# Rearranging all engines' work in the attention periods, the router stage and the first expert tile of a fused attention and mixture-of-experts kernel

## The chip, the cores and the metric

One core of a Trainium2 chip runs the whole kernel in one launch. The metric is the device time of that launch in microseconds. The kernel before takes 535.85 us, the median of three runs (535.5 to 536.07).

The core has engines that run side by side and meet only at semaphores: TensorE (PE; matrix products, transposes; writes only to PSUM banks), VectorE (DVE), ScalarE (ACT), GpSimd (POOL) and SyncE (SP), which here issues most of the transfers. Each engine works through its own list in order. A wait in such a list holds up everything behind it.

## The reference

Two steps are added to a residual stream `x` of 4 batches x 512 tokens x 512 channels. `ctx` holds 128 features for each token, `topk` keeps 153 of 512 values in a row.

```
sim  = (ctx @ Wq.T) (ctx @ Wk.T).T / scale            # per batch, 512 x 512
A    = sigmoid(sim) * (sim >= 153rd largest of its row)
x    = x + tanh(g1) * ((1-gamma) * layernorm(x) + gamma * (A + A.T) / 2)
xf   = layernorm(x)
shared = (silu(xf @ Gs.T) * (xf @ Ys.T)) @ Ds.T       # 704 hidden
s    = sigmoid(xf @ gate.T); two experts of 8 by s + bias, weights s/sum
out  = sum over the two: w_e * (silu(xf @ Ge.T) * (xf @ Ue.T)) @ De.T   # 352 hidden
x    = x + tanh(g2) * (shared + out)
```

`topk` must be exact, and the products are made to about float32's accuracy from pairs of float16 values, a high and a low half: high x high, high x low, low x high.

## The kernel before

The 2048 tokens are cut into 4 batches of 4 row tiles of 128. There is a prologue (attention of batch 0), then three calls of `together(b, more)`, one in each engine's list, then a last period with the router, then 39 expert tiles of 128 gathered token slots. In period `b` TensorE computes batch b's router logits (`logits`), its shared hidden blocks u = 0 to 5 (`shared_up`, 24 products of 512 columns each, 12 in block 5), and its shared down products (`shared_down`, one row tile at a time). Among these are the matrix turns for batch b + 1: `turn_attention` (the masked scores, which waits for `a_made`), `turn_batch` (a normalised row tile with its high and low half, into one of two banks, so tile 2 needs the bank of tile 0), and for batch b + 2 `project` and `scores`.

VectorE's list in period b: four rounds of a search for each row's threshold (`search`; ScalarE's `count` does half of the rows), exact thresholds by one more count and the eight largest below it (`last_counts`, `thresholds`), `count_missed`, `masks` (four `keep` instructions), `check`, which reads how many rows the search missed, branches to an exact fallback if there are any, and releases `a_made`; in between it multiplies the hidden blocks (`shared_hidden`, which frees TensorE's banks: block u + 2 waits for hidden block u). The first two base sums (`add_base`: gain x row + masked scores) stand inside `check` ahead of the branch. Then `attended` adds the turned scores, takes statistics, and makes the low half of each normalised row.

Weights arrive as 80 pieces of 128 x 544 float32 in a ring of four stage buffers (SP's `load_piece`, which waits until the low half of the piece four before is done). ScalarE makes the high half and scales the stage in place (`high_piece`), GpSimd or, for the last four experts, VectorE makes the low half (`low_piece`). `SLOT_PIECES` says how many pieces are handled at each hidden block u of periods 0 to 2. `high_piece` for slot u stands between the silu and the high half of block u or behind them, so a missing load holds ScalarE up with all its other work. GpSimd also makes the low half of each hidden block (`shared_low`) and the few scalars of a batch (`base_scalars`, `row_scalars`, `guess`).

In the last period VectorE chooses the experts (`choose`), counts (`count_tokens`), places the slots (`place`), builds one-hot matrices in eight steps (`hot_slots`), whose products with TensorE (`slots`) give the index table (`table`); `tile_experts` computes which expert each tile belongs to, and by how much the waits of the adding transfers count. GpSimd gathers four tiles' rows when `table` has released them. In an expert tile t ScalarE and VectorE alternate (silu, product, high half, low half), and in tiles 0 to 6 each converts four more weight pieces, two ahead of the high half and two at the end (`late_pieces`). TensorE's `turn_and_up` turns tile t - 1's hidden halves in the middle of tile t's products. The order of everything is written out by hand.

## Time and profile before

| | |
|---|---|
| median of three runs | 535.85 us |
| the profiled execution | 535.06 us, span 533.3 us |
| TensorE busy | 486.4 us, 91% of the span |
| VectorE, ScalarE, GpSimd busy | 327.7 us (61%), 254.3 us (48%), 220.4 us (41%) |
| transfers | 61.58 MB, mean 115 GB/s |
| share of the chain that ended last | TensorE 49%, VectorE 33%, ScalarE 5% |

TensorE's share is a mean over the whole span. The question in each stage is which wait ends last there. An order-of-time row has the start, the duration, the engine, the line of the kernel, the operation, what it writes and reads, and how many instructions it joins; square brackets hold the idle time of the engine ahead of it and who ended it. Rows of the same engine may overlap a little, since instructions are pipelined.

### The profile page before, as it was taken

How to read it: one execution, taken by the hardware profiler on the slowest of the kernel's cores; microseconds unless marked ns; L12 is line 12 of the kernel's file. 1: busy time of each engine (PE TensorE's matmuls, PEld its weight loads, DVE VectorE, ACT ScalarE, POOL GpSimd, SP SyncE). 2: the span in 40 equal slices, each digit the busy share in tenths (PEclk: the TensorE clock that was granted, in tenths of full speed). 3: DMA queues.
4: the chain of work that ended last, by engine and by line, in shares of the span. 5: the costliest groups of instructions: out<-in, count | busy, mean ns of one | idle time of the engine just before them, and what ended most of it. 6: DMA issues, size and time to landing. Idle time of an engine off the chain costs nothing.

```text
span 533.3 us, 10457 instructions
## 1 busy us (share of the span) xinstructions
PE 486.4 (91%) x2992; PEld 267.0 (50%) x2993; DVE 327.7 (61%) x726; ACT 254.3 (48%) x465; POOL 220.4 (41%) x229
## 2 busy tenths in 40 slices
PE   7467998999898997899889999999999999999991
PEld 2234433544344443454445666666666666666650
DVE  2999897899958995779976773323323233333330
ACT  3874696789389856532313653222222222222230
POOL 2022467616863296402430434443344443344322
PEclk9758798999999998999999999999999999999997
DMA  6430333354434442240056896566655666655643
GB/s 203 150 104 2 121 99 89 85 181 142 125 84 136 161 115 59 108 136 2 0 191 226 220 258 130 101 107 118 114 103 98 111 102 115 114 101 107 104 56 39
DMA packets 45478, 61.58 MB, mean 115 GB/s; under 512 B 20544, under 2 KB 20800, under 8 KB 45440
## 3 DMA queue, kind: packets, MB, share of 16 engines
q1 hardware_dynamic: 36272, 40.53, 25.7%
q0 software_dynamic: 8736, 20.45, 22.0%
q8 instruction: 18, 0.29, 0.2%
q10 hardware_dynamic: 432, 0.13, 0.1%
q14 instruction: 20, 0.16, 0.1%
HBM read 37.90 MB, written 19.14 MB: 107 GB/s over the span
## 4 chain that ended last, share of the span: by engine, by line
PE 49%; DVE 33%; issue 7%; ACT 5%; POOL 2%; DMA 2%; DVEq 0%; POOLq 0%; ACTq 0%
PE py L1153 14%; PE pg L1133 13%; PE pu L1134 13%; DVE w L1253 5%; PE pa L1143 2%; DVE work L1421 2%; DVE pa L1283 2%; DVE w L1310 2%; PE pt_bank L909 2%; DVE w L1300 2%; DVE w L1232 2%; DVE w L1287 1%; ACT w L688 1%; DVE w L1625 1%; DVE w L1359 1%
## 5 line engine op out<-in xcount | busy, mean ns | idle before, releaser
L1133 PE MATMUL pg<-w,x_t 128*128 x408 | 123.3, 313 | 0.0
L1134 PE MATMUL pu<-w,x_t 128*128 x408 | 123.2, 313 | 0.0
L580 POOL DMA_INDIRECT out<-rows,idx x39 | 61.8, 1586 | 134.3 <-issue 80.1
L975 PE MATMUL pg<-w 128*128 128x512 f16 x288 | 81.5, 402 | 6.0 <-DVE work L1421 6.0
L1153 PE MATMUL py<-w,work 128*128 x351 | 82.1, 379 | 0.8 <-DVE work L1688 0.8
L832 ACT ACTIVATE work<-pg 128x352 f32<-128x352 f32 x39 | 18.1, 463 | 120.0 <-PE pu L1134 120.0
L516 POOL TENSOR_TENSOR w<-stage,w 128x544 f16<-128x544 f32 x42 | 54.2, 1303 | 37.2 <-ACT stage L637 30.2
L975 PE MATMUL pu<-w 128*128 128x512 f16 x240 | 66.7, 388 | 0.0
L633 ACT ACTIVATE w<-stage 128x544 f16<-128x544 f32 x80 | 50.9, 648 | 28.3 <-DMA stage<-in_weights 28.0
L1677 DVE SCALAR_TENSOR_TENSOR work<-pu,work 128x352 f32<-128x352 f32 x39 | 20.4, 524 | 62.2 <-ACT work L832 56.8
L1688 DVE COPY work<-pa 128x768 f16<-128x768 f16 x39 | 21.8, 558 | 59.6 <-PE pa L1143 51.5
L1153 PEld LDWEIGHTS py<-w,work 128*128 128x128 f16 x351 | 34.3, 98 | 37.1 <-issue 1.2
L975 PEld LDWEIGHTS pg<-w 128*128 128x128 f16 x288 | 28.8, 102 | 42.2 <-issue 6.2
L1133 PEld LDWEIGHTS pg<-w,x_t 128*128 128x128 f16 x408 | 39.9, 98 | 17.5 <-issue 0.2
L530 POOL TENSOR_TENSOR work<-work 128x512 f16<-128x512 f32 x20 | 28.0, 1399 | 49.9 <-ACT work L714 49.9
L1134 PEld LDWEIGHTS pu<-w,x_t 128*128 128x128 f16 x408 | 39.9, 98 | 17.1
L975 PEld LDWEIGHTS pu<-w 128*128 128x128 f16 x240 | 23.9, 100 | 29.8 <-issue 2.7
L1253 DVE TENSOR_SCALAR_CACHE_REDUCE w<-w 128x512 f16<-128x512 f32 x48 | 33.9, 743 | 2.4 <-DVE w L1249 1.2
L1683 DVE TENSOR_TENSOR work<-work 128x352 f16<-128x352 f32 x39 | 20.4, 524 | 21.2 <-ACT work L837 21.2
L842 ACT ACTIVATE rows<-py,w_slot 128x512 f32<-128x512 f32 x39 | 26.8, 687 | 13.9 <-PE py L1153 13.9
L837 ACT ACTIVATE work<-work 128x352 f16<-128x352 f32 x39 | 19.3, 495 | 23.3 <-DVE work L1677 23.3
L1000 PE MATMUL pu<-w,work 128*128 128x512 f16 x120 | 27.8, 379 | 2.0 <-DVE w L1427 1.3
(250 smaller groups left out, 782.0 us busy)
## 6 DMA issues: line engine op xcount, KB each, us to landing
stage<-in_weights SPq DMA_DIRECT2D x80, 272.0 KB
xn_rows<-w SPq DMA_DIRECT2D x16, 256.0 KB, 2.8
out<-w SPq DMA_DIRECT2D x16, 256.0 KB, 2.5
w<-in_x SPq DMA_DIRECT2D x3, 1024.0 KB, 5.3
w<-in_ctx_t SPq DMA_DIRECT2D x4, 256.0 KB, 3.8
w<-in_x SPq DMA_DIRECT2D x2, 512.0 KB, 3.8
out<-rows,idx POOLq DMA_INDIRECT x39, 5.1
work<-xn_rows,idx POOLq DMA_INDIRECT x20
```

The source lines that it names most:

```text
L516: pool.tensor_tensor(w[:, ds(item, 1), 1, n * CHUNK_W:(n + 1) * CHUNK_W], stage[:, n % RING:n % RING + 1, :], w[:, ds(item, 1), 0, n * CHU ...
L530: pool.tensor_tensor(hid_tb[:, u, 1, :], hb[:, u % 2, :], hid_tb[:, u, 0, :], ALU.subtract).then_inc(hlo_sb, 1)
L580: pool.indirect_dma_start(out=out, out_offset=bass.IndirectOffsetOnAxis(ap=idx[:, t:t + 1], axis=0), in_=rows[:, t % 2, :], in_offset=None ...
L633: act.activation(w[:, ds(item, 1), 0, n * CHUNK_W:(n + 1) * CHUNK_W], stage[:, n % RING:n % RING + 1, :], ACT.Copy, scale=W_SCALE).then_in ...
L842: act.activation(rows[:, p, :], py[:, :], ACT.Copy, scale=w_slot[:, ds(t, 1)]).then_inc(y_sb, 1)
L975: mm = pe.matmul(bank_[:, :], w[:, half, part, at:at + P], x_tb[:, xpart * KC + k, :], start=(k, part, xpart) == (0, 0, 0), stop=(k, part) ...
L1000: pe.matmul(bank_[:, :], hid_tb[:, u, part, cols], w[:, half, wpart, at:at + C], start=(u, part, wpart) == (0, 0, 0), stop=False)
L1133: pe.matmul(pg[p][:, 0:H], lhs, w[:, item, half, at:at + H], start=begin, stop=end)
L1134: mm = pe.matmul(pu[p][:, 0:H], lhs, w[:, item, half, at + H:at + 2 * H], start=begin, stop=end)
L1153: mm = pe.matmul(py[:, :], hid_t[:, p, part * JC + j, :], w[:, item, half, at:at + C], start=(j, part, half) == (0, 0, 0), stop=(j, part) ...
L1253: o.mark(dve.tensor_scalar(junk[:, i, :], sim[:, i, :], cur[:, i:i + 1], 0.0, ALU.is_ge, ALU.add, accum_out=counts[:, i:i + 1]))
L1688: dve.tensor_copy(hid_t[:, p, :, :], hid_banks[p]).then_inc(ht_sb, 1)
```

## The change

The diff changes no computation. It changes the order in every engine's list:

- `SLOT_PIECES`: the numbers of weight pieces at blocks 0 to 5 in the three periods.
- GpSimd: in periods 1 and 2 `base_scalars` stands behind block 2's low half, not at block 1; at the end of a period two low pieces stand ahead of the first `row_scalars`.
- ScalarE: in period 0 the four `scaled_sigmoid` stand ahead of the first count. In the first expert tile all four pieces stand behind the hidden high half (VectorE's low pieces likewise), and so does the wait for the stored shared rows.
- TensorE: four products of zeros between the second and the third turn of batch 0; `turn_batch(b + 1, 1)` comes behind `shared_down(b, 2)`, `turn_batch(b + 1, 3)` in the middle of row tile 3's down products; in period 2 four of row tile 3's six blocks stand ahead of the turns of tiles 2 and 3, not three.
- VectorE: in periods 1 and 2 two masks ahead of hidden block 3 and two behind it, hidden block 4 between the read of the missed count and the branch, the base sums behind the release. In period 0 hidden block 2 ahead of the thresholds of tiles 2 and 3, hidden block 3 ahead of `count_missed`.
- The last period: hidden blocks 4 and 5 ahead of `tile_experts` and `hot_slots(5)`; behind the one-hot steps `shared_rows(3, 0)`, then `tile_experts`, then `table`; two low pieces ahead of `shared_rows(3, 1)`, not four.

```
-SLOT_PIECES = ((2, 2, 2, 2, 2, 3), (3, 3, 2, 0, 3, 3), (3, 3, 2, 0, 3, 2))
+SLOT_PIECES = ((2, 3, 3, 0, 0, 5), (4, 2, 2, 0, 1, 5), (4, 2, 2, 0, 1, 4))
+WARM_TURN = 4
 # GpSimd, together
-                    if u == (1 if b else 0):
+                    if u == 0 and b == 0:
                         base_scalars(b + 1)
...
+                    if u == 2 and b:
+                        base_scalars(b + 1)
                 last = slot_pieces(b, UPS - 1)
-                low_piece(*last[0])
+                for piece in last[:2]:
+                    low_piece(*piece)
                 row_scalars(b + 1, 0)
-                low_piece(*last[1])
+                low_piece(*last[2])
                 row_scalars(b + 1, 1)
-                for piece in last[2:]:
+                for piece in last[3:]:
 # ScalarE, together
-                count(b + 1, 0)
                 if b:
+                    count(b + 1, 0)
                     rows_turned(b, 3)
...
                 else:
+                    for i in range(TPB):
+                        scaled_sigmoid(b + 1, i)
+                    count(b + 1, 0)
                     keep_logits(b)
...
-                        if u in (1, 2):
-                            scaled_sigmoid(b + 1, 2 * u - 2)
-                            scaled_sigmoid(b + 1, 2 * u - 1)
 # ScalarE, expert tiles
                 silu(t, t % 2)
+                between = PER_TILE // 2 if t else 0
+                for piece in late_pieces(t)[:between]:
+                    high_piece(*piece)
+                hidden_high(t, t % 2)
                 if t == 0:
                     for s in sh_st:
                         after(act, s, TILES // 2 * 16)
-                for piece in late_pieces(t)[:PER_TILE // 2]:
-                    high_piece(*piece)
-                hidden_high(t, t % 2)
                 if t:
                     expert_rows(t - 1, (t - 1) % 2)
-                for piece in late_pieces(t)[PER_TILE // 2:]:
+                for piece in late_pieces(t)[between:]:
 # TensorE, prologue and together
-            for i in range(TPB):
-                turn_batch(0, i)
+            turn_batch(0, 0)
+            turn_batch(0, 1)
+            for n in range(WARM_TURN):
+                pe.matmul(py[:, :], zeros[:, 0:P], zeros[:, 0:512], start=True, stop=True)
+            turn_batch(0, 2)
+            turn_batch(0, 3)
...
                     turn_batch(b + 1, 0)
+                    shared_down(b, 2)
                     turn_batch(b + 1, 1)
-                    shared_down(b, 2)
                     turn_batch(b + 1, 2)
+                    shared_down(b, 3, range(0, 3))
                     turn_batch(b + 1, 3)
-                    shared_down(b, 3)
+                    shared_down(b, 3, range(3, UPS))
 # VectorE
+            def half_bases(b):
                 after(dve, base_ok, b + 1)
                 after(dve, xn_st, b * TPB * 16)
                 after(dve, xt_mm, b * TPB)
                 for i in range(TPB // 2):
                     o.mark(add_base(b, i))
+
+            def check(b, beside=None):
+                after(dve, miss_mm, b + 1)
+                o.then(dve.tensor_copy(missed_i[:], pa[0][0:1, 0:1]))
+                if beside is None:
+                    half_bases(b)
+                else:
+                    shared_hidden(b - 1, beside)
                 any_missed = dve.value_load(missed_i[0:1, 0:1], min_val=0, max_val=P * TPB)
...
                     count_missed()
-                    masks(b + 1, range(TPB))
+                    masks(b + 1, (0, 1))
                     shared_hidden(b, 3)
-                    check(b + 1)
-                    shared_hidden(b, 4)
+                    masks(b + 1, (2, 3))
+                    check(b + 1, 4)
+                    half_bases(b + 1)
                     shared_hidden(b, 5)
...
+                    shared_hidden(b, 2)
                     thresholds(b + 1, (2, 3))
-                    shared_hidden(b, 2)
+                    shared_hidden(b, 3)
                     count_missed()
-                    shared_hidden(b, 3)
 # VectorE, last period
                 if u == 4:
                     hot_slots(4)
-                    tile_experts(ends)
+                shared_hidden(BATCHES - 1, u)
                 if u == 5:
                     hot_slots(5)
-                shared_hidden(BATCHES - 1, u)
             for step in range(HOTS, SLOTS_STEPS):
                 hot_slots(step)
+            shared_rows(BATCHES - 1, 0)
+            tile_experts(ends)
             table()
-            for n in range(RING):
+            for n in range(2):
                 low_piece(LATE, n)
-            shared_rows(BATCHES - 1, 0)
             shared_rows(BATCHES - 1, 1)
-            for n in range(RING, CHUNKS - 2):
+            for n in range(2, CHUNKS - 2):
                 low_piece(LATE, n)
```

## Rows read from the trace of the kernel before

**Rows 1.** Order of time, TensorE, periods 0 to 2 (columns as explained above).
```profile
81.00 1.44 PE L975 MATMUL pg<-w 128*128 128x512 f16 x3 [2.33 <-DVE work L1421]
...
93.95 1.07 PE L904 MATMUL pa<-ident,w 128*128 128x128 f32 x8 [1.31 <-DVEq L1343]
...
115.88 0.96 PE L936 MATMUL pt_bank<-gw,w 128*128 128x16 f16 x32
...
144.71 4.45 PE L975 MATMUL pg<-w 128*128 128x512 f16 x12 [1.83 <-DVE work L1421]
...
164.19 0.61 PE L909 MATMUL pg<-ident,w 128*128 128x128 f16 x8 [0.77 <-DVE w L1377]
...
173.99 0.95 PE L936 MATMUL pt_bank<-gw,w 128*128 128x16 f16 x32
...
214.13 0.38 PE L996 MATMUL pu<-w,work 128*128 128x512 f16 x1 [1.89 <-POOL work L526]
...
228.91 0.95 PE L936 MATMUL pt_bank<-gw,w 128*128 128x16 f16 x32
```
**Rows 2.** Order of time, TensorE, twelve products of block 5 in period 3.
```profile
256.59 2.75 PE L975 MATMUL pg<-w 128*128 128x512 f16 x12
```
**Rows 3.** Stretches: bounds, length, busy time of each engine, granted clock, transfers.
```profile
143.00:149.00 6.00, 4.29 (x13) 1.59 (x14) 3.81 (x6) 2.98 (x6) 3.27 (x3) 0.72 0.16 47
207.00:229.00 22.00, 19.54 (x120) 9.87 (x119) 14.03 (x24) 14.59 (x22) 10.60 (x15) 1.00 0.27 97
```
**Rows 4.** Order of time, VectorE: masks (L1300) and hidden blocks (L1421).
```profile
84.41 1.40 DVE L1300 SCALAR_TENSOR_TENSOR w<-w,thr 128x512 f32<-128x512 f32 x2
88.55 0.69 DVE L1421 SCALAR_TENSOR_TENSOR work<-pu,work 128x512 f32<-128x512 f32 x1 [2.73 <-ACT work L708]
...
137.88 6.16 DVE L1300 SCALAR_TENSOR_TENSOR w<-w,thr 128x512 f32<-128x512 f32 x4
...
152.09 0.70 DVE L1421 SCALAR_TENSOR_TENSOR work<-pg,work 64x512 f32<-64x512 f32 x1 [5.02 <-ACT work L708]
```
**Rows 5.** Order of time, ScalarE: first count (L674), first normalised rows (L688).
```profile
59.94 0.72 ACT L674 ACTIVATE w<-w 128x512 f16<-128x512 f32 x1 [2.88 <-DVEq L1264]
...
101.87 0.81 ACT L688 ACTIVATE w<-w,pt 128x512 f32<-128x512 f32 x1 [0.36 <-POOLq L509]
...
159.98 0.81 ACT L688 ACTIVATE w<-w,pt 128x512 f32<-128x512 f32 x1 [1.23 <-POOLq L509]
```
**Rows 6.** Order of time, ScalarE and GpSimd: weight pieces in period 1.
```profile
138.00 0.66 ACT L633 ACTIVATE w<-stage 128x544 f16<-128x544 f32 x1 [3.41 <-DMA stage<-in_weights]
...
134.01 3.57 POOL L516 TENSOR_TENSOR w<-stage,w 128x544 f16<-128x544 f32 x3 [0.38 <-ACT w L633]
```
**Rows 7.** Order of time, VectorE: seven instructions of `tile_experts`.
```profile
256.36 2.92 DVE L1597 SCALAR_TENSOR_TENSOR rc<-iota_col,re,rc 1x39 f32<-1x39 f32 x7
```
**Rows 8.** Order of time, TensorE, period 3 and the first expert product.
```profile
266.45 0.38 PE L996 MATMUL pu<-w,work 128*128 128x512 f16 x1 [1.70 <-POOL work L526]
...
273.42 3.41 PE L1000 MATMUL pu<-w,work 128*128 128x512 f16 x15 [1.33 <-DVE w L1427]
...
277.30 0.62 PE L909 MATMUL pt_bank<-ident,work 128*128 128x128 f16 x8
...
282.07 0.32 PE L1133 MATMUL pg<-w,x_t 128*128 x1
```
**Rows 9.** The first gather's issue; packets, MB of the gathers' queue, 271 to 274.
```profile
269.88 1.23 POOL L575 DMA_INDIRECT work<-xn_rows,idx  x1 [3.58 <-DVEq L1634]
...
q0 software_dynamic: 80, 0.26, 30.9%
```
**Rows 10.** Order of time, first expert tiles: TensorE, ScalarE, VectorE.
```profile
289.00 0.49 PE L1143 MATMUL pa<-ident,work 128*128 128x128 f16 x6 [0.94 <-DVE work L1683]
...
302.58 1.32 ACT L633 ACTIVATE w<-stage 128x544 f16<-128x544 f32 x2 [2.32 <-DMA stage<-in_weights]
...
287.06 1.36 DVE L1216 SCALAR_TENSOR_TENSOR w<-stage,w 128x544 f16<-128x544 f32 x2
```
**Rows 11.** Order of time, TensorE: third turn of batch 0 in the prologue.
```profile
52.20 0.61 PE L909 MATMUL pt_bank<-ident,w 128*128 128x128 f16 x8 [1.95 <-DVE w L1377]
```

More of the change, by code:

```diff
@@ L1053, in together @@
                     turn_batch(b + 1, 1)
-                    shared_down(b, 3, range(0, 3))
+                    shared_down(b, 3, range(0, 4))
                     turn_batch(b + 1, 2)
                     turn_batch(b + 1, 3)
-                    shared_down(b, 3, range(3, UPS))
+                    shared_down(b, 3, range(4, UPS))
             for b in range(BATCHES - 1):
@@ L1311, in add_base @@
                                                 in1=kept[:, i, :], op0=ALU.mult, op1=ALU.add)
-            def check(b):
-                after(dve, miss_mm, b + 1)
-                o.then(dve.tensor_copy(missed_i[:], pa[0][0:1, 0:1]))
+            def half_bases(b):
                 after(dve, base_ok, b + 1)
@@ L1339, in check @@
                         f.then(keep(b, i))
-                        if i < TPB // 2:
+                        if i < TPB // 2 and beside is None:
                             f.then(add_base(b, i))
@@ L1711, in _ @@
                 hidden(t, t % 2)
-                for piece in late_pieces(t)[:PER_TILE // 2]:
+                between = PER_TILE // 2 if t else 0
+                for piece in late_pieces(t)[:between]:
                     low_piece(*piece)
@@ L1716, in _ @@
                 hidden_turned(t, t % 2)
-                for piece in late_pieces(t)[PER_TILE // 2:]:
+                for piece in late_pieces(t)[between:]:
                     low_piece(*piece)
```

## The prediction

> **What bounds the kernel now.** I read the table of busy shares first, then the granted clock by stretch, then TensorE's order of time, and for each of its gaps the engine that ended it, in that engine's order of time. The reader is to see that TensorE is busy in most of the span, that from 282.07 us, where the first expert tile begins [rows 8], it goes on to the end, and that the change touches only the first tiles of that stage. So the question is when that tile begins. Ahead of it lie four periods: period 0 up to 115.88, period 1 up to 173.99, period 2 up to 228.91, then period 3 [rows 1]. In period b TensorE works on batch b's shared hidden blocks 0 to 5 while VectorE masks batch b + 1's attention.
>
> TensorE's gaps there: 2.33 and 1.31 us in period 0; 1.83 and 0.77 in period 1; 1.83 once more (the same pattern) and 1.89 in period 2 [rows 1]; 1.70 and 1.33 in period 3 [rows 8]. The gap of 1.83 costs more than itself: the twelve products after it take 4.45 us, twelve at full rate 2.75 [rows 1, 2], and the granted clock of the stretch is 0.72 [rows 3]. That is another 1.70 us, in two periods.
>
> VectorE or a chain through it ends nearly all of them. In period 1 four masks stand ahead of hidden block 3, which frees TensorE; they take 6.16 us, 1.54 each beside GpSimd's work, where two others take 0.70 each [rows 4]. In period 0 it sits idle for 2.73 us ahead of hidden block 4, and its release of attention is then what TensorE waits for. In period 1 it sits idle for 5.02 us ahead of the last hidden block [rows 4], because ScalarE has three weight pieces to do between block 4 and the silu of block 5.
>
> **The change, part by part.** Times in the changed kernel are on the old time axis, less what was won before.
>
> *Period 0.* Hidden block 2 goes ahead of two thresholds, so TensorE's block 4 starts where block 3 ends, at 81.00 - 2.33 = 78.67. VectorE's work stays the same, and of its time only the idle 2.73 can be saved: it releases attention at 93.95 - 2.7 = 91.2. TensorE arrives 2.33 and some slow products earlier, at about 88.5, and waits there longer than now; whether the clock falls in that wait is worth 0 to 1.7 us (the price in period 1). The four sigmoids go into ScalarE's idle of 2.88 ahead of the first count [rows 5] and fill it: cost 0 to 0.1. Behind the copy of the projection ScalarE gets four pieces for two. A piece is two activations of 0.66 that overlap a little [rows 6], 1.24, so 2.5 us more, of the 2.7 that the projection is early; with one wait for GpSimd less, the first normalised row starts at about 101.0 against 101.87 [rows 5]. Then row tile 2's turn must wait until VectorE has emptied tile 0's bank: that copy comes after all four low rows, 1.2 us earlier than now, while TensorE comes 2.7 earlier. So 1.5 of what TensorE wins ends as a wait there. Net: 1.2 won if the clock holds, 0.5 lost if it falls. I take +0.5 (bounds -0.7 and +2.7).
>
> *Period 1.* Two masks fewer ahead of hidden block 3: even at 1.54 a mask it comes 3.1 us before its place behind the masks, 137.88 + 6.1 = 144.0, so at 140.9. TensorE, which is ready at 144.71 - 1.83 = 142.88, less the 1.2 that period 0 may give, no longer waits: 1.83 and 1.70 go. What is queued behind the check's wait for the missed count is hidden block 4, needed by attention anyway, and TensorE has its block 5 of 2.6 us and six products of 1.3 to do meanwhile. The two base sums move behind the release, two of 0.7 (or 1.54) beside those: no cost; without that cover up to 3.1. GpSimd's base scalars move behind its third low half and still end ahead of the base sums; the pieces of slot 1 come earlier by their length, and ScalarE's wait of 3.41 for a load goes, since the load was released by a low half at 134.01 + 1.19 = 135.2 [rows 6]. One piece for three in slot 4 takes 2.5 us out of the idle ahead of the last hidden block. It is paid with four pieces behind the projection's copy. The first row starts at 155.5 against 159.98, of which ScalarE waited 1.23 [rows 5]; the wait of 0.77 at row tile 1 goes with its later turn, and at tile 2 it grows by 0.7. So 1.83 + 1.70 + 0.77 - 0.7 = 3.6; 0.5 off for a clock that may fall there: +3.1 (bounds 1 and 4.3).
>
> A rule weighed: the page "SBUF — State Buffer" of the Trainium skill, section "SBUF: two separate sides", says that a VectorE instruction with two SBUF inputs and a GpSimd instruction take a shared pair of ports in turn, each whole. The masks of 1.54 against 0.70 agree with it. By the rule the pieces and low halves that move beside the masks and the count hold up each of these anew, and the gain of the earlier hidden block could be lost in both periods: that is rival D.
>
> *Period 2.* The same 1.83 + 1.70, and 1.89, the wait for GpSimd's last low half [rows 1]: it follows the last hidden block, which wins the 2.5 of two pieces on top of TensorE's. Together 5.4. No scores are made here, and ScalarE stood idle ahead of its rows, so nothing that I see is late next: +5.4 (bounds 3 and 6).
>
> *Period 3.* The tile table's small instructions, seven of them 2.92 us and all about 4 (3.2 without the last one's delay beside GpSimd), leave their place ahead of hidden block 4 [rows 7]. The block comes 2.4 earlier, when its silu is done: 1.70 goes. The last one-hot steps follow without them, the first shared row is stored ahead of the index table: 1.33 goes. But those 3.2 us and the row's 0.7 now stand ahead of the index table, of whose old place some 2.3 are won: indices 1.6 us later, and the four gathers behind them on GpSimd. TensorE wants the first gathered tile 3.1 earlier than 277.30, at 274.2 [rows 8]. The trace has the first gather's issue at 269.88 and 0.26 MB, one tile of 128 rows, through by 274.0 [rows 9]; by 277.30 it had surely landed, since no wait stands there. So it lands at 275.6 to 278.9, and costs 1.4 to 4.7; I take 1.5, by the packets. Net 1.70 + 1.33 - 1.5 = +1.5 (bounds -1.7 and +3).
>
> *First expert tile.* Its four pieces go behind both hidden halves, so the gap of 0.94 [rows 10] shrinks to 0.3: +0.6. But the stage ring has four places. The low halves that free it ran from 287.06; now they come behind the hidden low half, the gathered copy and the turned copy of the tile (0.5, 0.7 and 0.5, after some waiting), by my estimate from 289.5: the loads for tile 1 go out 2.4 later. A load took 138.00 - 135.2 = 2.8 from its release [rows 6], and in this stage one kept ScalarE waiting 2.32 more [rows 10]. Piece 12 so comes at 293.0 to 295.3; ScalarE wants it at 291.1, ahead of tile 1's high half, and TensorE has 1.1 us of room: a wait of 0.9 to 3.1, I take 2.1. Net -1.5 (bounds +0.6 and -3).
>
> *Zero products.* Four of about 0.43 at the slow rate, 1.7, inside a gap of 1.95 [rows 11]: nothing on the path. If they keep the clock up, TensorE's first blocks are sooner, but block 2 waits for hidden block 0, whose place on VectorE does not move. 0 (bounds -0.5 and +0.5).
>
> **Sum.** 0.5 + 3.1 + 5.4 + 1.5 - 1.5 + 0 = 9.0 us. The profiled execution took 535.06 us (span 533.3 and 1.8 around it), 0.8 under the median of 535.85. 535.06 - 9.0 = 526.1; on the median, 526.9.
>
> **Rivals.**
> *A, new waits and a falling clock.* At the release in period 0 and at tile 2's turn in periods 0 and 1 the clock falls, 1.7 each, 5.1, of which 1.2 are counted: 3.9 more, 530.8. For: the gap of 1.83 lowered it. Against: one of 1.89 lies in a stretch of clock 1.00 [rows 3].
> *B, all gaps go.* Clock held (0.7 and 0.5), gathers in time (1.5), no wait for the ring (2.1): 4.8 better, 522.1. Against: each has only 0.5 to 1 us of room.
> *C, slower.* The ring of pieces never catches up, and each of tiles 1 to 5 waits as tile 1 does. Ahead of them 10.5 + 0.6 = 11.1 are won; five waits of 2.2 use them up, and from there on the kernel is slower; at 3.1, 15.5, it is 535.85 + 4.4 = 540.3. For: loads already end ScalarE's waits there. Against: TensorE waits nowhere in those tiles now, and each of its waits gives the loads the same time.
> *D, the masks stay late.* Contention moves with GpSimd's pieces, and hidden block 3 still comes after TensorE: 3.5 less in each of two periods, 533.9.
>
> **How the numbers follow.** Forecast 0.50, A 0.20, B 0.14, D 0.10, C 0.06. This measurement can tell 0.2%, 1.1 us, from no change. The forecast's own range is 523 to 530.5; that of 8 in 10 takes in most of A and of B: 521 to 532. Faster by over 0.2%: the forecast, A, B and half of D, 0.89; within: 0.04 of D; slower: C and the last of D, 0.07.
>
> **What would show it.** Right: no gap ahead of block 5 in periods 1 and 2, and a clock near 1.00; period 3 begins near 219; a wait at the first gathered tile; tile 1's high half behind a load. Wrong: hidden block 3 still releases block 5 (D); gaps in each tile from 1 to 5 (C); the first expert tile later than 276, or period 1 begins later than before.

## The result, and the profile after

The changed kernel takes 529.79 us (median of four runs, 529.21 to 531.43) beside 535.67 for the kernel before (four runs, 535.38 to 536.07): ratio 0.988, 95% interval [0.986, 0.990]. The forecast was 526.9, its range 521 to 532. The profiled execution took 531.43 us, span 529.6; it was the slowest of the four, so the stages below add up to a win of 3.7 us, where the medians give 5.9. The stages by TensorE's order of time, before [rows 1, 8, 10] and after (us):

| stage | begins before | begins after | length before | after | won | forecast |
|---|---|---|---|---|---|---|
| period 0 | 53.68 | 54.19 | 62.20 | 61.87 | 0.3 | 0.5 |
| period 1 | 115.88 | 116.06 | 58.11 | 55.79 | 2.3 | 3.1 |
| period 2 | 173.99 | 171.85 | 54.92 | 49.54 | 5.4 | 5.4 |
| last period, router | 228.91 | 221.39 | 53.16 | 53.60 | -0.4 | 1.5 |
| tiles 0 to 4, to tile 5's turn | 282.07 | 274.99 | 38.45 | 41.62 | -3.2 | -1.5 |
| from tile 5's turn on | 320.52 | 316.61 | 212.8 | 213.0 | -0.2 | 0 |

(Period b begins with batch b's logits. Why the prologue ran 0.5 longer I didn't follow up; in later executions with the same prologue period 0 began anywhere from 53.2 to 55.6.) The kernel after, TensorE's order of time, periods 0 to 2:

```profile
91.51 1.06 PE L909 MATMUL pa<-ident,w 128*128 128x128 f32 x8 [1.58 <-DVEq L1359]
...
104.76 0.61 PE L914 MATMUL pt_bank<-ident,w 128*128 128x128 f16 x8 [1.31 <-DVE w L1393]
...
111.16 0.61 PE L914 MATMUL pt_bank<-ident,w 128*128 128x128 f16 x8 [1.47 <-DVE w L1429]
...
116.06 0.96 PE L941 MATMUL pt_bank<-gw,w 128*128 128x16 f16 x32
...
146.88 1.04 PE L909 MATMUL pa<-ident,w 128*128 128x128 f32 x8
...
160.51 0.61 PE L914 MATMUL pt_bank<-ident,w 128*128 128x128 f16 x8 [1.07 <-DVE w L1393]
...
166.96 0.61 PE L914 MATMUL pt_bank<-ident,w 128*128 128x128 f16 x8 [1.51 <-DVE w L1429]
...
219.22 0.61 PE L914 MATMUL pt_bank<-ident,w 128*128 128x128 f16 x8 [0.54 <-DVE w L1429]
```

The gaps of 1.83 ahead of block 5 and of 1.89 in period 2 [rows 1] are gone: masked scores are turned at 146.88 with nothing waited for. What is left is mainly a wait for the release (1.58, period 0) and, in both periods 0 and 1, waits at the turns of tiles 1 and 2. VectorE in period 1 (masks L1310, hidden blocks L1437, base sums L1320) shows why:

```profile
139.86 1.41 DVE L1310 SCALAR_TENSOR_TENSOR w<-w,thr 128x512 f32<-128x512 f32 x2
141.19 0.68 DVE L1437 SCALAR_TENSOR_TENSOR work<-pu,work 128x512 f32<-128x512 f32 x1
141.79 1.40 DVE L1310 SCALAR_TENSOR_TENSOR w<-w,thr 128x512 f32<-128x512 f32 x2
...
144.77 2.36 DVE L1320 SCALAR_TENSOR_TENSOR w<-w,pt 128x512 f32<-128x512 f32 x2 [0.41 <-issue]
```

Hidden block 3 starts at 141.19 (forecast 140.9), and the four masks take 2.81 us where they took 6.16 [rows 4]: GpSimd now does its small scalars beside them instead of a piece. ScalarE's first normalised row comes at 102.30 and 157.73, against 101.87 and 159.98 [rows 5]; the fourth piece behind the projection's copy waits for its load in both periods:

```profile
99.61 0.66 ACT L637 ACTIVATE w<-stage 128x544 f16<-128x544 f32 x1 [0.77 <-DMA stage<-in_weights]
...
102.30 0.82 ACT L692 ACTIVATE w<-w,pt 128x512 f32<-128x512 f32 x1
...
155.05 0.66 ACT L637 ACTIVATE w<-stage 128x544 f16<-128x544 f32 x1 [0.86 <-DMA stage<-in_weights]
...
157.73 0.82 ACT L692 ACTIVATE w<-w,pt 128x512 f32<-128x512 f32 x1
```

Granted clock by stretch (columns as in [rows 3]): 80 to 90 and 140 to 150 are now at full rate, where the kernel before had 0.83 in both; in 250 to 262 and 289 to 297 it falls, and in the latter the kernel before had 1.00.

```profile
80.00:90.00 10.00, 9.56 (x45) 4.02 (x43) 9.68 (x17) 5.25 (x10) 6.84 (x6) 1.00 0.40 115
140.00:150.00 10.00, 10.00 (x55) 5.36 (x54) 9.01 (x13) 5.84 (x10) 7.92 (x9) 1.00 0.13 37
...
250.00:262.00 12.00, 9.85 (x62) 5.30 (x61) 9.87 (x18) 4.58 (x8) 3.81 (x3) 0.90 0.00 0
...
289.00:297.00 8.00, 7.28 (x43) 4.22 (x44) 5.92 (x11) 4.56 (x9) 2.63 (x2) 0.79 0.81 206
```

TensorE in the last period and the first tiles, answering [rows 8, 10]. The gaps of 1.70 and 1.33 are gone; two new ones stand at the last one-hot steps (L1090), the fifteen products behind them take 4.61 us where fifteen took 3.41 [rows 8], and the gathered tile (its turn is the L914 row) is waited for 0.45. Turns of the hidden halves are L1153.

```profile
258.44 0.45 PE L1090 MATMUL pa<-w 128*128 128x156 f16 x4 [1.04 <-DVE w L1642]
259.99 0.70 PE L1090 MATMUL pa<-w 128*128 128x156 f16 x4 [1.10 <-DVE w L1642]
260.49 4.61 PE L1005 MATMUL py<-w,work 128*128 128x512 f16 x15
...
269.95 0.61 PE L914 MATMUL pt_bank<-ident,work 128*128 128x128 f16 x8 [0.45 <-issue]
...
281.26 0.49 PE L1153 MATMUL pa<-ident,work 128*128 128x128 f16 x6 [0.28 <-DVE work L1700]
...
289.72 0.49 PE L1153 MATMUL pa<-ident,work 128*128 128x128 f16 x6 [1.99 <-DVE work L1700]
```

ScalarE and VectorE of the kernel after in tiles 0 and 1 (pieces L637 and L1226, the hidden high half L841). The four pieces wait for the stored shared rows, the loads that their low halves release come late, and tile 1's high half stands behind them. GpSimd's next gather (L579) waits for the same stores:

```profile
281.85 2.30 ACT L637 ACTIVATE w<-stage 128x544 f16<-128x544 f32 x4 [1.29 <-DMA out<-w]
...
286.13 0.66 ACT L637 ACTIVATE w<-stage 128x544 f16<-128x544 f32 x1 [1.64 <-DMA stage<-in_weights]
287.72 0.66 ACT L637 ACTIVATE w<-stage 128x544 f16<-128x544 f32 x1 [0.93 <-DMA stage<-in_weights]
288.29 0.48 ACT L841 ACTIVATE work<-work 128x352 f16<-128x352 f32 x1
```
```profile
282.54 2.63 DVE L1226 SCALAR_TENSOR_TENSOR w<-stage,w 128x544 f16<-128x544 f32 x4 [0.19 <-ACT w L637]
```
```profile
282.65 1.44 POOL L579 DMA_INDIRECT work<-xn_rows,idx  x1 [7.50 <-DMA out<-w]
```

### The profile page after: what moved, and what is told of

Its sections match the earlier page's. It is cut to its first block, busy times and chain, and to the rows that moved or that the text cites. A ratio compares the mean times of both kernels' runs of the same rounds, so it can differ in the third digit from the quotient of the medians.

```text
span 529.6 us, 10465 instructions
## 1 busy us (share of the span) xinstructions
PE 488.6 (92%) x2996; PEld 268.4 (51%) x2997; DVE 326.2 (62%) x726; ACT 255.1 (48%) x465; POOL 219.9 (42%) x229
## 4 chain that ended last, share of the span: by engine, by line
PE 64%; DVE 17%; ACT 6%; DMA 6%; issue 4%; POOL 2%; DVEq 0%; ACTq 0%; POOLq 0%; SPq 0%
PE py L1163 14%; PE pu L1144 12%; PE pg L1143 12%; PE pg L980 8%; PE pu L980 7%; DMA stage<-in_weights 3%; PE pa L1153 2%; DVE w L1263 2%; PE pt_bank L914 2%; ACT w L692 2%; PE py L1005 1%; DVE w L1320 1%; DVE pa L1293 1%; ACT w L637 1%; DVE w L1242 1%
## 5 line engine op out<-in xcount | busy, mean ns | idle before, releaser
L980 PE MATMUL pg<-w 128*128 128x512 f16 x288 | 77.5, 385 | 0.0
L517 POOL TENSOR_TENSOR w<-stage,w 128x544 f16<-128x544 f32 x42 | 55.3, 1334 | 36.1 <-ACT stage L641 29.3
L637 ACT ACTIVATE w<-stage 128x544 f16<-128x544 f32 x80 | 50.8, 649 | 29.9 <-DMA stage<-in_weights 28.0
L531 POOL TENSOR_TENSOR work<-work 128x512 f16<-128x512 f32 x20 | 26.2, 1312 | 42.0 <-ACT work L718 41.4
L841 ACT ACTIVATE work<-work 128x352 f16<-128x352 f32 x39 | 19.3, 495 | 23.7 <-DVE work L1694 23.7
L579 POOL DMA_INDIRECT work<-xn_rows,idx x20 | 20.7, 1034 | 22.3 <-DVEq L1651 9.3
```

Of the source, the lines that this page charges most:

```text
L517: pool.tensor_tensor(w[:, ds(item, 1), 1, n * CHUNK_W:(n + 1) * CHUNK_W], stage[:, n % RING:n % RING + 1, :], w[:, ds(item, 1), 0, n * CHU ...
L531: pool.tensor_tensor(hid_tb[:, u, 1, :], hb[:, u % 2, :], hid_tb[:, u, 0, :], ALU.subtract).then_inc(hlo_sb, 1)
L579: pool.indirect_dma_start(out=xg_slots[slot], out_offset=None, in_=xn_rows, in_offset=bass.IndirectOffsetOnAxis(ap=idx[:, t:t + 1], axis=0 ...
L637: act.activation(w[:, ds(item, 1), 0, n * CHUNK_W:(n + 1) * CHUNK_W], stage[:, n % RING:n % RING + 1, :], ACT.Copy, scale=W_SCALE).then_in ...
L980: mm = pe.matmul(bank_[:, :], w[:, half, part, at:at + P], x_tb[:, xpart * KC + k, :], start=(k, part, xpart) == (0, 0, 0), stop=(k, part) ...
```

## Experiments

Each was timed against the kernel before on the same chip; stage lengths come from one profiled execution of each. Four chips were used, on which the kernel before had medians of 537.25, 537.99, 536.64 and 536.59 us, so ratios are compared, not times.

**1. First expert tile's pieces two and two, as before** (run twice, and the changed kernel again between).

```
-                between = PER_TILE // 2 if t else 0
+                between = PER_TILE // 2
```

> The changed kernel with one part undone: in expert tile 0 two weight pieces stand ahead of the high half and two at the end, on ScalarE and VectorE, as before. Theory (the ring): deferring all four made the next tile's loads late, so tile 1's turn waits 1.99 us and its clock falls for some 1.7 more; undone, that gap goes, the 0.94 gap in tile 0 comes back for 0.28, and the kernel takes 526 to 527.5 us. Rival (tile 1 waits because the stage itself begins 7 us earlier than the loads can follow): the gap at tile 1 stays over 1 us and the time stays at 529 to 531.

> The changed kernel itself once more, so that the runs beside it have it on the same chip: 0.982 to 0.989 of the kernel before. What differs between its two profiles is to tell how much of tile 1's loss is the clock.

> The changed kernel with the first expert tile's four pieces two and two, as before, once more, beside the two versions that build on it. Theory (the ring's places come free in time, so tile 1 doesn't wait, and the clock holds there): ratio to the kernel before 0.978 to 0.983, no gap at any tile's turn, 38.4 us from the first expert product to tile 5's turn. If the gap at tile 1 had gone by chance in the first run: a gap of about 2 us at tile 1's turn again, and 0.984 to 0.986.

Measured: 0.981 [0.978, 0.983] and 0.983 [0.981, 0.986] with the edit undone; the changed kernel again 0.984 [0.982, 0.987], in its first timing 0.988 [0.986, 0.990]. The intervals of neighbours overlap, so the traces have to decide. With two and two, first expert product to tile 5's turn takes 38.45 and 38.76 us (38.45 in the kernel before), and the only gap of note is the old 0.94 at tile 0's turn. In the changed kernel it takes 41.62, 40.19 when run again, and 39.58 in experiment 2's kernel without zero products, which is the same from here on. So four behind costs 0.8 to 3.2 us. The difference between the changed kernel's two executions is the clock. In the first, tile 2's turn follows tile 1's after 7.97 us; in the second, whose gap was longer, after 6.30, at full rate:

```profile
289.31 0.49 PE L1153 MATMUL pa<-ident,work 128*128 128x128 f16 x6 [2.25 <-DVE work L1700]
...
295.61 0.50 PE L1153 MATMUL pa<-ident,work 128*128 128x128 f16 x6
```
```profile
289.00:297.00 8.00, 7.69 (x61) 5.07 (x62) 6.42 (x12) 5.17 (x9) 3.21 (x3) 1.00 0.87 241
```

The first trace with two and two also tells what bounds the last period, whose order in it is the changed kernel's. There the clock held at the one-hot steps, though the gaps were the same, 1.04 and 1.11, and the fifteen products took 3.40. Nothing was won by it: TensorE waited 1.73 at the turn of the gathered tile instead of 0.45, and the period took 53.61 us for 53.60. The profile names no releaser for this wait, but the gather's packets pass between 267 and 270.

```profile
269.81 0.61 PE L914 MATMUL pt_bank<-ident,work 128*128 128x128 f16 x8 [1.73 <-issue]
```

**2. VectorE's order of the last period as before; and no zero products.** The first puts `tile_experts` back ahead of hidden block 4 and `hot_slots(5)` ahead of block 5, `table()` with four low pieces ahead of the first shared row, and leaves the first expert tile's four pieces behind; the second is `WARM_TURN = 0`.

> The changed kernel with VectorE's order of the last period put back: tile table ahead of hidden block 4, one-hot step 5 ahead of hidden block 5, first shared row behind the index table and four low pieces. Theory (the last period lost as much as it won: 53.60 us from its logits to the first expert product, 53.16 before): the old gaps of 0.63, 1.70 and 1.33 come back, the new ones at the last one-hot steps (1.04, 1.10, with 1.2 of slow products behind) go, and the time is within 0.7 us of the changed kernel, 529.1 to 530.5. Rival (the part is worth the 1.5 us of the prediction and the rest was chance): 531 to 532.

> The changed kernel without the four products of zeros in the prologue. Theory (period 0 is bound by VectorE and ScalarE): TensorE's first blocks stay at the slow rate as now (the clock was 0.76 over 40 to 60 us in both kernels), period 1 begins within 0.3 us of 116.06, and the time is the same, 529.4 to 530.2. Rival (they hold the clock up or delay the turns): a change of 1 us or more.

Measured: 0.984 [0.980, 0.987] and 0.984 [0.981, 0.987]. With the old order the gaps of 1.71 and 1.33 are back and the new ones gone; the last period takes 53.83 us against 53.60: inside it the rearrangement is worth 0.2. But it costs more behind it. With the old order the last shared rows are stored sooner after the stage begins, no wait stands ahead of the four pieces, and the gap at tile 1's turn is 0.83, not 1.99; the tiles to tile 5's turn take 38.78 us.

```profile
280.53 0.95 POOL L579 DMA_INDIRECT work<-xn_rows,idx  x1 [4.29 <-PE pt_bank L914]
```
```profile
289.38 0.49 PE L1153 MATMUL pa<-ident,work 128*128 128x128 f16 x6 [0.83 <-DVE work L1700]
```

So the late return of the ring's buffers makes a gap of 0.83 at tile 1 by itself. The rest in the changed kernel goes with the late stores, along two ways. The low halves come 7.55 us behind the first expert product instead of 7.27. And the gather, issued 7.66 us behind the first expert product instead of 4.72, moves its 0.26 MB between 285 and 287, beside the loads; the second load then takes 3.7 us from issue to landing, where it takes 2.9 here and in experiment 5, whose gather is early too. Together these come near the difference of 1.16; no run moves the gather alone.

Without zero products the third turn waits 1.95, as in [rows 11], and period 0 takes 61.45 us against 61.87 and 62.06. TensorE's first products of period 0 run at the lower of its two levels with them and without them (1.44 us for three). So no gain shows; that they cost the 0.4 to 0.6 isn't shown either, since with them this period took from 61.5 to 62.1 in six executions and 63.9 in a seventh.

**3. Only the masks, the check and the base sums, on the kernel before.**

```
-                    masks(b + 1, range(TPB))
+                    masks(b + 1, (0, 1))
                     shared_hidden(b, 3)
-                    check(b + 1)
-                    shared_hidden(b, 4)
+                    masks(b + 1, (2, 3))
+                    check(b + 1, 4)
+                    half_bases(b + 1)
```

> The kernel before with only this part of the change: in periods 1 and 2 two masks ahead of hidden block 3 and two behind, hidden block 4 between the read of the missed count and the branch, base sums behind the release. Weight pieces, base scalars and TensorE's order are the old ones. Theory (these hold most of what periods 1 and 2 won): the gap of 1.83 and the slow clock after it go in both periods, 3 us in each at most; as the three pieces ahead of the last silu stay, the last hidden block stays late and some of it ends in a wait behind attention: 530 to 532.5 us. Rival (the pieces and the base scalars won it, by contention or by the loads): the gap of block 5 stays over 1 us, 534 to 536.

Measured: 0.992 [0.989, 0.994]. The gap ahead of block 5 and its slow products are gone in both periods, but period 1 takes 56.59 us (1.5 won) and period 2 takes 53.69 (1.2 won), of 3.5 each. The time comes back further on in TensorE's order of time, three rows of period 1 and one of period 2, where the wait for GpSimd's last low half has grown from 1.89 to 3.38 and the fifteen products behind it take 4.72 for 3.41:

```profile
152.94 1.13 PE L890 MATMUL pu<-w 128*128 128x512 f32 x2 [1.25 <-ACT w L650]
...
162.59 0.61 PE L909 MATMUL pg<-ident,w 128*128 128x128 f16 x8 [0.98 <-DVE w L1383]
...
167.99 0.61 PE L909 MATMUL pt_bank<-ident,w 128*128 128x128 f16 x8 [1.02 <-DVE w L1419]
...
210.80 0.44 PE L996 MATMUL pu<-w,work 128*128 128x512 f16 x1 [3.38 <-POOL work L526]
```

So this edit alone is worth 2.7 us of the 7.7 that periods 1 and 2 win. The rest needs the other parts, the pieces, the base scalars and the turns' new places; what each of them brings was not measured. Here the masks still took 2.99 and 2.67 a pair beside GpSimd's old order, and block 5 waited for nothing even so.

**4. A more even deal of pieces.** In periods 0 and 1 two pieces, in period 2 one, moved from behind the last block to earlier ones.

```
-SLOT_PIECES = ((2, 3, 3, 0, 0, 5), (4, 2, 2, 0, 1, 5), (4, 2, 2, 0, 1, 4))
+SLOT_PIECES = ((2, 3, 3, 1, 1, 3), (4, 2, 2, 2, 1, 3), (4, 2, 2, 1, 1, 3))
```

> The changed kernel with the weight pieces dealt differently: ((2,3,3,1,1,3), (4,2,2,2,1,3), (4,2,2,1,1,3)), so three instead of five (or four) at the last hidden block, the others at block 3, where ScalarE now waits 3.52 us for hidden block 3. Theory (the tail): in periods 0 and 1 ScalarE's four pieces behind the projection's copy set when the normalised rows come, and with them the gaps of 1.31, 1.47, 1.07 and 1.51 us at the turns; without two of them those gaps go, period 1 begins 2 to 2.8 us earlier, period 2 4 to 5.3 earlier than in the changed kernel, and the ratio to the changed kernel is 0.990 to 0.993. Rival (the gaps at the turns come from TensorE's new order and VectorE's single copy behind four low rows): they stay over 0.8 each and the ratio is 0.997 to 1.001.

Measured: 0.991 [0.987, 0.994], above the changed kernel's 0.984 [0.982, 0.987] on the same chip, so slower than either expectation. ScalarE is free earlier, but GpSimd must make the low halves then. VectorE's masks and base sums in period 0, and GpSimd's pieces and then its row scalars (L506), ScalarE's row and the turn that waits, in period 1:

```profile
85.95 2.08 DVE L1310 SCALAR_TENSOR_TENSOR w<-w,thr 128x512 f32<-128x512 f32 x2
...
90.05 3.09 DVE L1320 SCALAR_TENSOR_TENSOR w<-w,pt 128x512 f32<-128x512 f32 x2
```
```profile
145.44 3.30 POOL L517 TENSOR_TENSOR w<-stage,w 128x544 f16<-128x544 f32 x2
...
156.21 0.19 POOL L506 TENSOR_SCALAR pt<-mv 128x2 f32<-128x2 f32 x1
```
```profile
157.76 0.81 ACT L692 ACTIVATE w<-w,pt 128x512 f32<-128x512 f32 x1 [2.66 <-POOLq L510]
```
```profile
167.35 0.79 PE L914 MATMUL pt_bank<-ident,w 128*128 128x128 f16 x8 [2.32 <-DVE w L1429]
167.93 3.65 PE L1005 MATMUL py<-w,work 128*128 128x512 f16 x9
```

A pair of masks took 1.42 in the changed kernel, the base sums 2.13; beside GpSimd's pieces they take 1.6 us longer in all, and the release came at 93.34. The Trainium skill ("SBUF — State Buffer", "SBUF: two separate sides") says that a VectorE instruction with two SBUF inputs and a GpSimd instruction that reads SBUF take their shared ports in turn; these lengths agree with it. In period 0 this was paid back: the turns waited 0.34 in place of 1.31 and 1.47, and the period took 61.29 us for 61.87. The loss is in period 1, 58.11 us for 55.79: GpSimd reaches its row scalars late, the turn of tile 2 waits 2.32, and the nine products behind it take 3.65, where nine at full rate take 2.12. The expert tiles lost as well, 42.60 us to tile 5's turn, with a gap of 2.96 at tile 1's.

**5. The index table first, one-hot step 5 early.** `hot_slots(5)` ahead of hidden block 4, and the half of `table` that makes the gathers' indices ahead of `tile_experts`.

```
-            tile_experts(ends)
-            table()
+            table(lambda: tile_experts(ends))
```

> The changed kernel with two edits in the last period: one-hot step 5 stands ahead of hidden blocks 4 and 5, and the index half of the table stands ahead of the tile table (TensorE then waits for the table's second half). Theory: the gaps of 1.04 and 1.10 at the last one-hot steps and the slow clock behind them (15 products in 4.61 us in place of 3.41) come from step 5 being late; they shrink to 0.5 together, the wait of 0.45 at the first gathered tile goes, and the first expert product comes 2.5 to 3.5 us earlier: 0.993 to 0.996 of the changed kernel. Rival (the gathers and the loads of the late weights then end last): the first expert product is under 1.5 us earlier or tile 1 loses more than it does now.

Measured: 0.983 [0.980, 0.985], not to be told from the changed kernel's 0.984. The last period takes 52.59 us, 1.0 less, where 2.5 to 3.5 were expected. Indices are there at 258.63, 38.3 us into the period and not 42.9, the gathered tile is not waited for, one gap of 0.79 is left at the one-hot steps, and the fifteen products behind it take 3.40. But TensorE, done at 270.57, then waits 2.35 for shared row 2, which VectorE had behind two pieces whose loads were late:

```profile
269.73 0.72 DVE L1226 SCALAR_TENSOR_TENSOR w<-stage,w 128x544 f16<-128x544 f32 x1 [1.13 <-ACT w L637]
270.37 0.69 DVE L1709 COPY x_t<-pt_bank 128x1024 f16<-128x1024 f16 x1
270.97 0.74 DVE L1443 SCALAR_TENSOR_TENSOR w<-pu,cst,w 128x512 f32<-128x512 f32 x1
```
```profile
272.93 0.32 PE L1143 MATMUL pg<-w,x_t 128*128 x1 [2.35 <-issue]
```

Behind that wait the clock fell: from the first expert product to tile 0's turn it took 7.95 us, in the changed kernel 6.27, which takes back the 1.0. Its tile 1 agrees with experiment 2's: here too the shared rows were stored in time, the four pieces started at 280.08 with no wait, the gather was issued at 278.08, and the gap at tile 1's turn is 0.91, not 2.

**6. Experiments 1, 4 and 5 together.**

> All of it together: the changed kernel with the pieces of the first expert tile as before the change, the pieces dealt as in the run with three at the last block, step 5 early and the index half first. If the terms add, 3 to 4 us at tile 1, 3 to 5 in periods 0 and 1, 2.5 to 3.5 in the last period: 518 to 522 us beside 529.8, 0.968 to 0.975 of the kernel before. If the late weights' loads become the bound, tile 1 to 5 show waits of over 1 us each and the sum falls short by 3 us or more.

Measured: 0.990 [0.987, 0.993], where 0.968 to 0.975 was expected if the terms add. The deal of experiment 4 costs what it did there (period 1 took 58.09), and the wait of experiment 5 grew to 4.56, behind a piece whose load was later still.

**7. Experiments 1 and 5, and shared row 2 ahead of the late pieces.** The loop over pieces 2 to 5 ends at 3; 4 and 5 go behind gathered tile 0's copy and shared row 2.

```
-            for n in range(2, CHUNKS - 2):
+            for n in range(2, RING):
                 low_piece(LATE, n)
             gathered_turned(0, 0, 0)
             shared_rows(BATCHES - 1, 2)
-            for n in range(CHUNKS - 2, CHUNKS):
+            for n in range(RING, CHUNKS):
                 low_piece(LATE, n)
```

> Four edits on the changed kernel: the first expert tile's pieces two and two again; one-hot step 5 ahead of hidden block 4; the index half of the table ahead of the tile table; and, new, gathered tile 0's copy and shared row 2 ahead of the low pieces 4 and 5, which wait for loads. Theory: in the run without the last edit TensorE was done with its down products at 270.57 and began the first expert product at 272.93, because shared row 2 stood behind two low pieces whose loads were late; so that wait of 2.35 shrinks to 0.5 or less. The last period takes 50.6 to 51.2 us (53.6 in the changed kernel), the expert tiles 38.4 to the turn of tile 5, and the kernel about 522.5 to 525: ratio to before 0.973 to 0.977. Rival 1 (the wait is the gathered tile or the tile table, not the shared row): the last period stays at 52.5, ratio 0.977 to 0.980. Rival 2 (pieces 4 to 7 now come too late for tiles 0 and 1): gaps at the turns of tiles 0 and 1 of 1 us or more, and nothing won over the version with pieces two and two alone.

Measured: 523.41 us, 0.975 [0.973, 0.978]: the fastest of all, 0.9 to 1.3% below the changed kernel's two ratios. The last period takes 50.16 us. Shared row 2 now runs at 267.84, and the first expert product follows the last down product without a gap:

```profile
270.82 0.39 PE L1002 MATMUL py<-w,work 64*128 64x512 f16 x1
271.14 0.32 PE L1143 MATMUL pg<-w,x_t 128*128 x1
...
278.07 0.49 PE L1153 MATMUL pa<-ident,work 128*128 128x128 f16 x6 [0.94 <-DVE work L1699]
```

**8. One piece moved in periods 0 and 1; then in period 0 alone, with one piece of tile 0 early and three late.**

```
+SLOT_PIECES = ((2, 3, 3, 0, 1, 4), (4, 2, 2, 0, 2, 4), (4, 2, 2, 0, 1, 4))
```
```
+SLOT_PIECES = ((2, 3, 3, 0, 1, 4), (4, 2, 2, 0, 1, 5), (4, 2, 2, 0, 1, 4))
+                between = PER_TILE // 2 if t else 1
```

> The same four edits, and one piece moved from behind the projection's copy to block 4 in periods 0 and 1: SLOT_PIECES ((2, 3, 3, 0, 1, 4), (4, 2, 2, 0, 2, 4), (4, 2, 2, 0, 1, 4)). Theory (ScalarE's fourth piece, 1.24 us and its late load, delays the first normalised row and so the turns of tiles 2 and 3): the rows start 1 us earlier, the gaps of 1.3 and 1.5 at these turns lose 1 us in each of two periods, 2 us in all, ratio 0.969 to 0.974. Rival (what one period's piece costs GpSimd beside the masks is what counts, as where two were moved): the release of attention in period 0 or the row scalars in period 1 come later by 0.5 to 1 us, and the kernel is 0 to 2 us slower than without this edit.

> The version of four edits (pieces two and two in the first expert tile, one-hot step 5 early, index half first, shared row 2 ahead of the late pieces), with two smaller ones: the piece moved from behind the projection's copy to block 4 in period 0 alone, SLOT_PIECES ((2, 3, 3, 0, 1, 4), (4, 2, 2, 0, 1, 5), (4, 2, 2, 0, 1, 4)), and in the first expert tile one piece ahead of the hidden high half and three behind, not two and two. Theory: in the version that moved the piece in both periods, period 0 took 0.8 us less and period 1 1.2 more than without; so the move in period 0 alone wins 0.8. One piece ahead takes the gap of 0.94 at tile 0's turn to 0.3, and tile 1 doesn't wait: 0.6 more. In all 1.4 off, ratio to before 0.971 to 0.974, the turn of tile 5 near 308.5. Rival (the ring has less than a piece's 1.2 us of room at tile 1): a gap of 0.5 us or more at tile 1's turn, which gives back what tile 0 won. If period 0's 0.8 was the scatter of loads: period 0 takes 61.5 us again, and ratio 0.974 to 0.977.

Measured: 0.978 [0.975, 0.981] and 0.979 [0.976, 0.981], neither better than experiment 7. Period 0 takes 60.75 and 60.76 us for its 61.52, so there the piece is worth 0.8; but with the move in period 0 alone, period 1 takes 56.39 for 55.97, and with the move in both 57.16, so the move in period 1 costs 0.8 to 1.2. With one piece early in tile 0 the rival held. TensorE's gap of 0.94 at tile 0's turn is gone, and 2.50 stand at tile 1's; ScalarE waited 3.15 for the stored rows with three pieces behind that wait, and VectorE 1.49 for these pieces:

```profile
279.51 1.75 ACT L637 ACTIVATE w<-stage 128x544 f16<-128x544 f32 x3 [3.15 <-DMA out<-w]
...
284.60 0.66 ACT L637 ACTIVATE w<-stage 128x544 f16<-128x544 f32 x1 [2.44 <-DMA stage<-in_weights]
```
```profile
286.59 0.49 PE L1153 MATMUL pa<-ident,work 128*128 128x128 f16 x6 [2.50 <-DVE work L1699]
```

## Why the prediction was right, and where its terms were off

The direction held, and so did the mechanism in periods 1 and 2, which hold most of the win; the last period and the first expert tile went otherwise than forecast. The forecast was 2.9 us too low. By the number alone rival A, 530.8, was nearer, and the range of 8 in 10 took A in. By mechanism the kernel is not A's: the clock held at the three waits that A names, and fell at two others, in the router stage and at tile 1. Part of the 2.9 is scatter: timed again, the changed kernel won 9.0 us (528.98 beside 537.99), the forecast's own figure, though not by its terms.

*Period 0 (+0.5; +0.3).* The release came at 91.51 (forecast 91.2), TensorE waited 1.6 for it at full clock. So 1.2 should have been won, by the sum's own terms. The first normalised row came at 102.30, not 101.0: the fourth piece waited 0.77 for its load, and tile 1's turn waited 1.31, which was not in the sum. I had taken 0.7 off for a clock that held; that the two errors nearly cancel is luck. The sign that I had named against this step, a period 1 that begins later than before, did show (116.06 for 115.88), but by a prologue that ran 0.5 longer.

*Period 1 (+3.1; +2.3).* The 1.83 and the 1.70 went, as experiment 3 shows for that edit alone, and the clock held. The turn of tile 2 waits 1.51, where the kernel before waited 0.66: a growth of 0.85 for the 0.7 forecast. The term that was mis-sized is tile 1's turn: 1.07, where I had none. So 3.6 - 1.07 - 0.15 = 2.4, without the 0.5 that I took off for a clock that held. ScalarE's row ahead of that turn came at 157.73, not 155.5: 0.86 of that is the load of the fourth piece, and the rest is that the copy ahead of the four pieces, at 149.75, came 4.35 earlier than before and not the 5.7 that my row implies.

*Period 2 (+5.4; +5.4).* Right in its total: period 3 began at 221.39 (by the sum 219.9, given as near 219; of the 1.5 between, 0.5 is the prologue, 0.2 period 0 and 0.8 period 1). But experiment 3 shows that of the 3.5 that I put to the earlier block, 1.2 comes by itself: with the old deal of pieces the last low half comes as late as before, and TensorE waits for it 3.38. The terms of this sum are not independent, as I had them.

*Last period (+1.5; -0.4).* This step failed, and the term that was mis-sized is the gathered tile. I had the indices 1.6 us later and 1.5 for the wait. In the trace they are written 42.86 us into the period, where the kernel before had them at 39.73: 3.1 later. The tile table and the shared row ahead of them take the 3.9 that I gave them, but their place came 0.8 earlier and not 2.3. Where the clock holds (experiment 1), TensorE turns the gathered tile at 269.81, 48.4 us into the period, the same as before the change (277.30), so nothing is left of the 1.70 and 1.33. The wait in the changed kernel's profile, 0.45, only looks cheap, because TensorE came late to it. `hot_slots(5)` went behind hidden block 5, so that three one-hot steps stand there, not two, and TensorE outruns VectorE at the last two: 1.04 and 1.10, and slow products for another 1.2, none of which was in the sum. They are not a second price: with the clock up, the 1.2 turn into a longer wait for the tile (1.73). The first expert product waits another 0.2 to 0.35. Experiment 5, which has the indices early and step 5 early, has no wait for the tile, one gap of 0.79 and no slow products; step 5 alone was not run, and by the traces of experiment 1 it would win nothing while the indices are late.

*First expert tile (-1.5; -3.2).* The figures of the chain came out to a tenth: low halves at 282.54, where my 289.5 less the 7.1 won gives 282.4; the late load served at 286.13 and 287.72 in the forecast span of 285.9 to 288.2; the gap 1.99 for 2.1; tile 0 won 0.66 for 0.6. But the gap's size is luck. By the ring alone, which is all that the forecast reckons with, it is 0.83 or 0.91 (experiments 2 and 5), the low end of my 0.9 to 3.1; the other 1.1 goes with the late stores, which I did not see, and which hold up ScalarE's pieces (1.29) and a gather whose packets then meet the loads. The last kernel of experiment 8 shows a gap of 2.50 behind a wait of 3.15. And the clock fell in that gap, 1.67 more, in one execution of two. Two and two wins it all back (experiment 1).

*Zero products (0; 0).* Right as far as it can be told (experiment 2).

*Rivals.* B did not come: the load waits and the turns stayed. C did not: tiles 2 to 5 wait nowhere. D did not: the masks took 0.70 each, since GpSimd's scalars stand beside them. Nor would it have with slow masks, since in experiment 3 they took 2.99 and 2.67 a pair and hidden block 3 still came in time. Contention itself is right in kind: in experiment 4 two masks took 0.7 longer and two base sums 1.0 where a piece does stand there.

## What to carry to other kernels

When work is moved off a late step, follow each engine that takes it over to what stands behind it: here five gaps of 1.3 to 1.9 us went, but pieces put behind a copy delayed the rows, an index table put behind other work made TensorE wait for the gather that follows it, and four pieces moved late, with a store's wait ahead of them, cost 0.8 to 3.2 us one tile later. A late store also releases whatever else waits for it: here a gather then ran beside the loads on which the next tile hung. In a list run in order, the step that another engine waits for goes ahead of any step that may itself wait for a load: that one swap was worth 2.4 us (experiment 7's last period beside experiment 5's). With few ring buffers look at the moment at which a buffer is given back, and not only at the moment at which its content is used.

## What was not expected of the hardware

A gap does not cost the same each time. After 1.99 us TensorE's products started 0.29 us apart in place of 0.15, the lower of its two levels (1.2 GHz), and cost 1.67 more; after 2.25 in another execution of the same kernel, and after 2.50 in experiment 8's last one, they went on at 2.4 GHz. So did those after 1.52 at the same turn (experiment 2), while 2.96 there (experiment 4) and 2.35 ahead of the first expert product (experiment 5) lowered the level. Two gaps of 1.04 and 1.10 with only four products between them lowered it in both profiles of the changed kernel (fifteen products in 4.61 and 5.09 us for 3.40), but not in experiment 1's two, with 1.04 and 1.11 at the same steps. The length of the gap alone doesn't decide; what does stays open.
